# Mamba head stage: squares summed per group on GpSimd, output products one head later, decay clamp on VectorE, six biased exponentials on ScalarE

## The reference

```
proj  = x @ in_proj_w.T                      # gate, hidden, B, C, dt
hbc   = silu(causal conv of 4 taps + bias)   # hidden -> X, B, C
dt    = softplus(dt + dt_bias);  A_bt = -exp(A_log) * dt
L     = exp(cumsum difference of A_bt), lower triangle
y     = (C B^T * L) @ (X * dt) + D * X       # written in chunks in the reference
g     = y * silu(gate)
g     = g * rsqrt(mean over the group's 512 channels of g*g + 1e-6)
x     = layernorm(x + (norm_w * g) @ out_proj_w.T)
```

## Time and profile before

| what | us |
|---|---|
| median of three executions | 3315.8 |
| the three | 3315.8, 3317.79, 3304.01 |
| the profiled execution | 3299.21 |
| its span in the profile | 3297.4 |
| PE busy in the span | 2619.4 (79%) |
| DVE busy | 1809.8 (55%) |
| ACT busy | 1525.4 (46%) |
| POOL busy | 1227.2 (37%) |

### The profile page before, as it was taken

The page is one execution under the profiler, slowest core; times in us unless marked ns, Lnnn a source line. Parts: engine busy times, 40 slices in busy tenths (PEclk is TensorE's granted clock), DMA queues, the critical chain, the costliest instruction groups (busy, mean ns, idle before and its releaser), DMA issues. The chain is left out here.

```text
span 3297.4 us, 47157 instructions
## 1 busy us (share of the span) xinstructions
PE 2619.4 (79%) x13661; PEld 1670.5 (51%) x13663; DVE 1809.8 (55%) x3839; ACT 1525.4 (46%) x2975; POOL 1227.2 (37%) x1164
## 2 busy tenths in 40 slices
PE   4799999987999996577777937878557749698884
PEld 2467777744777775344444523333244414365552
DVE  4666666674666664788882146776223342133234
ACT  3555555564555552588891114655235410233321
POOL 0477777635777773000000020000000027344443
PEclk8999999998999997666657957999679868799997
DMA  1121211002221210740000000000000024587885
GB/s 61 52 52 33 59 48 36 14 14 58 58 52 33 58 26 26 250 136 1 1 1 31 0 18 1 1 1 1 23 0 0 0 81 158 129 177 172 175 172 126
DMA packets 127073, 192.74 MB, mean 58 GB/s; under 512 B 17552, under 2 KB 88208, under 8 KB 125584
## 3 DMA queue, kind: packets, MB, share of 16 engines
q1 hardware_dynamic: 83696, 134.71, 14.5%
q0 software_dynamic: 23616, 33.24, 5.8%
q10 hardware_dynamic: 19584, 22.57, 2.5%
HBM read 123.23 MB, written 67.25 MB: 58 GB/s over the span
## 5 line engine op out<-in xcount | busy, mean ns | idle before, releaser
L234 DVE SCALAR_TENSOR_TENSOR h_pre<-h_px,h_par,h_pre 128x510 f32<-128x510 f32 (+2 forms) x384 | 286.5, 746 | 269.1 <-ACT h_pre L695 249.2
L658 PE MATMUL h_po<-h_wo,h_h 128*128 128x256 f32 x1024 | 328.2, 411 | 0.0
L580 POOL TENSOR_SCALAR h_decay<-h_cumb,h_sel 128x256 f32<-128x256 f32 x256 | 290.9, 1136 | 25.2 <-DMA h_cumb<-cum_rows 25.2
L591 POOL TENSOR_TENSOR h_mix<-h_decay,cb 128x768 f32<-128x768 f32 x128 | 232.8, 1819 | 165.0 <-ACT h_decay L681 165.0
L2890 POOL DMA_INDIRECT moe_sums<-ex_y,ex_sidx x132 | 204.8, 1552 | 234.7 <-DVE ex_y L3069 216.6
L622 PE MATMUL h_px<-x_cols,h_w 128*128 128x512 f32 x512 | 254.4, 620 | 25.3 <-DMA h_d<-d_skip 25.3
L849 POOL TENSOR_TENSOR norm_rstd<-norm_mv,mhalf 128x4 f32<-128x4 f32 x24 | 28.3, 1178 | 605.3 <-DVE norm_mv L832 605.3
L627 PE MATMUL h_pz<-x_cols,h_w 128*128 128x512 f32 x512 | 242.5, 596 | 5.6 <-DVE h_gate L748 5.6
L707 ACT ACTIVATE h_xt<-h_pxt,h_sel 128x128 f32<-128x128 f32 x512 | 145.9, 368 | 151.9 <-PE h_pxt L646 151.9
L2942 PE MATMUL ex_pg<-ex_w,ex_xT 128*128 x528 | 194.7, 492 | 25.6 <-ACT ex_xT L2998 10.5
L660 PEld LDWEIGHTS h_pss<-ones,h_sq 128*128 128x128 f32 x1024 | 194.6, 190 | 26.3
(11 more groups left out here) (389 smaller groups left out, 5809.6 us busy)
## 6 DMA issues: line engine op xcount, KB each, us to landing
h_cumb<-cum_rows SPq DMA_DIRECT2D x32, 1024.0 KB, 8.6
moe_tiles<-blank SPq DMA_DIRECT2D x4, 6642.0 KB, 44.2
ex_w<-moe_w SPq DMA_DIRECT2D x64, 352.0 KB
ex_xg<-moe_tiles ACTq DMA_DIRECT2D x136, 162.0 KB, 2.6
ex_wd<-moe_wd SPq DMA_DIRECT2D x64, 176.0 KB
h_w<-w_xg SPq DMA_DIRECT2D x8, 1024.0 KB, 10.5
moe_sums<-blank SPq DMA_DIRECT2D x2, 2176.0 KB, 26.6
h_wo<-w_out SPq DMA_DIRECT2D x8, 512.0 KB, 10.3
```

The costliest lines, as they stand in the source:

```text
L234: ins = dve.scalar_tensor_tensor(out=out[:, :, back:S], in0=src[:, :, 0:S - back], scalar=par[:, at + CK - 1 - back:at + CK - back], in1=o ...
L580: pool.tensor_scalar(decay[j][:, u, 0:S], cumb[s.vb][:, j, u, :], sel[s.vb][:, u * TPB, 1, j:j + 1], 0.0, ALU.subtract, ALU.min)
L591: pool.tensor_tensor(mix[j % 2][:], decay[j][:], cbj, ALU.mult).then_inc(matched, 1)
L658: pe.matmul(po[t // TPB][:, t % TPB, :], hh[j % 2][:, t * P:(t + 1) * P], w_out[s.pg][:, j, :], start=(j == 0 and t % TPB == 0), stop=(j = ...
```

## The change

The loops and LEAD go: all 64 slots of a half are written out, and a wait whose count would be zero or less is left out (`after`). The memsets of `h_po` and `h_pss` go with them. The rest moves work between engines and slots:

- Squares: ACT squares head 0 of a step into `h_sqs` and the others into `h_sq`; POOL adds the three into `h_sqs` (`total`, 128x512); PE then makes one set of four one-column products per step.
- Output: PE's `out` goes from head k to head k-1; `h_h` gets four buffers instead of two; `out` no longer waits for a square.
- Variance and addition of the step before go from slot j = 0 to slot j = 1, the addition to the end of that slot.
- Decay: DVE takes the minimum of the broadcast sums and the row's own sum on the two diagonal blocks (`argue`, one 128x512 instruction); ACT takes six exponentials of 128 columns with the negated row sum as bias (`h_less`, made in `select`), and reads the off-diagonal block directly from `h_cumb`.
- POOL scales `h_wo` half a group ahead, for the first group before anything else.

```diff
-            parts = ((3, project), (1, scan), (2, turn), (0, out))
+            parts = ((3, project), (1, scan), (2, turn), (-1, out))
+            head_slots(-3, 1, lambda k: slot(parts, k))
...
             def out(s, j, h):
-                pe.wait_ge(finished, LEAD + h + 1)
-                pe.wait_ge(squared, LEAD + h + 1)
+                pe.wait_ge(finished, h + 1)
                 if j == 0:
-                    pe.wait_ge(added, LEAD + s.n)
-                    pe.wait_ge(scaled, LEAD + s.g + 1)
+                    after(pe, added, s.n)
+                    pe.wait_ge(scaled, s.g + 1)
                 for t in range(TW):
-                    pe.matmul(po[t // TPB][:, t % TPB, :], hh[j % 2][:, t * P:(t + 1) * P], w_out[s.pg][:, j, :],
-                              start=(j == 0 and t % TPB == 0), stop=(j == HG - 1), skip_group_check=True)
-                    mm = pe.matmul(pss[:, t:t + 1], sq[j % 2][:, t * P:(t + 1) * P], r.ones[:, 0:1],
-                                   start=(j == 0 and t == 0), stop=(j == HG - 1), skip_group_check=True)
+                    mm = pe.matmul(po[t // TPB][:, t % TPB, :], hh[j][:, t * P:(t + 1) * P], w_out[s.pg][:, j, :],
+                                   start=(j == 0 and t % TPB == 0), stop=(j == HG - 1), skip_group_check=True)
                 mm.then_inc(outed, 1)
+                if j == HG - 1:
+                    pe.wait_ge(totalled, (s.n + 1) * (HG - 1))
+                    after(pe, vared, s.n)
+                    for t in range(TW):
+                        mm = pe.matmul(pss[:, t:t + 1], sqs[s.vb][:, t * P:(t + 1) * P], r.ones[:, 0:1], start=True, stop=True)
+                    mm.then_inc(pooled, 1)
...
+            def total(s, j, h):
+                if j:
+                    pool.drain()
+                    pool.wait_ge(squared, h + 1)
+                    pool.tensor_tensor(sqs[s.vb][:], sqs[s.vb][:], sq[j % 2][:], ALU.add).then_inc(totalled, 1)
...
             def decays(s, j, h):
-                act.wait_ge(argued, LEAD + h + 1)
-                act.activation(decay[j][:], decay[j][:], ACT.Exp).then_inc(decayed, 1)
+                act.wait_ge(argued, h + 1)
+                for u in range(2):
+                    act.activation(decay[j][:, u, P:S], cumb[s.vb][:, j, u, P:S], ACT.Exp, bias=less[s.vb][:, u * TPB, j:j + 1])
+                    for b in range(TPB):
+                        own = decay[j][:, u, 2 * b * P:(2 * b + 1) * P]
+                        ins = act.activation(own, own, ACT.Exp, bias=less[s.vb][:, u * TPB + b, j:j + 1])
+                ins.then_inc(decayed, 1)
...
+            def argue(s, j, h):
+                dve.wait_ge(cums[s.vb], (s.g * (NP // 2) + s.two + 1) * 16)
+                after(dve, matched, h - HG + 1)
...
+                dve.tensor_tensor(own, cum, lim, ALU.min).then_inc(argued, 1)
...
-            def body(prev, cur, nxt):
-                for j in range(HG):
-                    finish(*head(cur, nxt, j))
-                    if j == 0:
-                        variance(prev)
-                    slot(((2, silu),), cur, nxt, j)
-                    if j == 0:
-                        if nxt:
-                            select(nxt)
-                        add(prev)
-                    slot(((3, conv), (3, open_)), cur, nxt, j)
+            def body(k):
+                n, j = divmod(k, HG)
+                slot(((0, finish), (2, silu)), k)
+                if j == 0 and n + 1 < len(STEPS):
+                    select(STEPS[n + 1])
+                if j == 1 and n >= 1:
+                    variance(STEPS[n - 1])
+                slot(((3, conv), (3, open_), (3, argue)), k)
+                if j == 1 and n >= 1:
+                    add(STEPS[n - 1])
```

More of the change, by code:

```diff
@@ L414, with __init__, head_slots, at_head @@
 class Step:
[L417 to L442, removed]
+    def __init__(self, n):
+        self.n = n
+        self.g, self.p = divmod(n, NP)
+        self.g2, self.pg = divmod(self.g, 2)
+        self.two, self.vb = divmod(self.p, 2)
+STEPS = [Step(n) for n in range(GH * NP)]
+def head_slots(first, last, body):
+    for k in range(first, len(STEPS) * HG + last):
+        body(k)
+def at_head(h):
+    return (STEPS[h // HG], h % HG, h) if 0 <= h < len(STEPS) * HG else None
 def mamba_heads(nc, a, r, half, cum_rows, dtc, cb):
@@ L522, in mamba_heads, with slot, group @@
         block = ctx2.enter_context(nc.Block())
[L524 to L529, removed]
+        def slot(parts, k):
             for ahead, part in parts:
-                at = head(cur, nxt, j + ahead)
-                if at:
-                    part(*at)
+                if at_head(k + ahead):
+                    part(*at_head(k + ahead))
         @block.sync
         def _(sp):
-            def group(g2, pg):
-                sp.wait_ge(added, LEAD + (g2 * 2 + pg - 1) * NP)
-                g = (g2 * 2 + pg) * 2 + half
+            def group(s):
+                pg = s.pg
+                after(sp, added, (s.g - 1) * NP)
+                g = s.g * 2 + half
                 sp.dma_start(w_in[pg][:], a["w_xg"][g]).then_inc(loaded[pg], 16)
@@ L573, in group @@
                                    ALU.mult).then_inc(scaled, 1)
[L575 to L584, removed]
@@ L606, in _ @@
[L606 to L609, removed]
+            def body(k):
+                if k % (HG * NP) == HG * NP // 2 and k // HG + NP // 2 < len(STEPS):
+                    group(STEPS[k // HG + NP // 2])
+                slot(((2, match), (-1, total)), k)
+                if k % HG == 1 and k > HG:
+                    root(STEPS[k // HG - 1])
+            group(STEPS[0])
@@ L611, in _ @@
+            head_slots(-2, 1, body)
+            root(STEPS[-1])
         @block.tensor
         def _(pe):
[L613 to L614 removed]
             def project(s, j, h):
[L617 removed]
+                if s.p == 0 and j == 0:
                     pe.wait_ge(loaded[s.pg], (s.g2 + 1) * 64)
[L620 removed]
+                after(pe, convolved, h - 1)
@@ L689, in activate @@
+            def square(s, j, h):
+                act.wait_ge(finished, h + 1)
+                if j == 0:
+                    after(act, pooled, s.n - 1)
+                    act.activation(sqs[s.vb][:], hh[j][:], ACT.Square).then_inc(squared, 1)
+                else:
+                    after(act, totalled, s.n * (HG - 1) + (0, 0, -1, 1)[j])
+                    act.activation(sq[j % 2][:], hh[j][:], ACT.Square).then_inc(squared, 1)
             def activate(s, j, h):
-                if s.opens and j == 0:
+                if s.p == 0 and j == 0:
```

146 lines of the change are left out of this document (59 added, 87 removed).

## The result

| | us, median | lowest to highest | runs |
|---|---|---|---|
| before, beside it | 3313.78 | 3304.01 to 3318.04 | 10 |
| after | 3330.74 | 3324.33 to 3336.10 | 10 |

The ratio is 1.0056, 95% interval [1.0043, 1.0068]: slower by 0.56%, 17 us. The profiled execution took 3328.39 us, with a span of 3326.4 (3297.4 before).

The account below looks back on a forecast made before the run. PE alone was taken to set the pace in the head stages. Work, waits, filling and tail gave -9 us, half clock +24, so +15 on the median 3315.8: forecast 3330 us, likeliest case 3313 to 3347, 8-in-10 range 3288 to 3375.

Parts of the forecast that it names:

- PE's work: In the head stages, slots shorten from 7.80 to 6.94 us, plus 0.86 per step; alone, 32 steps give back 83 us.
- The wait: PE's first output product of a step waits 2.82 us for DVE's late addition, eating the whole gain.
- The chain: From a slot's first projection through tap, conv, gate, minimum and addition until PE starts: 8.08 us.
- What is hidden: ACT's six exponentials (0.285 each), DVE's minimum and POOL's adds fit beside PE's slot; at worst 10 us in all.
- The clock: PE runs at half clock after half of the 28 stream waits, adding 24 us; the ends are none and 48.
- B: Every PE wait is followed by half clock: 3355 us, up to 3390; chance 0.24.
- C: PE's wait is there but its clock never falls: 3307 us; chance 0.15.
- D: PE's wait is absent or short: 3228 us, or 3268 with half of it; chance 0.16.
- Filling and tail: At each half's start and end: filling 7.1 us shorter, tail 1.7 us longer.
- the wait of step 15: The last step's PE wait, left out of the 14 counted per half because it lies in the tail.
- Rival E: POOL blocks DVE's minimum through SBUF reads, making the wait 4.6 us with half clock each time: 3406 us; chance 0.03.

Follow-up runs that it names:

- the fifth experiment: Changed kernel with output, sums, variance and addition in their old slots, addition ahead of conv, and one-column products per head without POOL's sums: 3297.14 us, 0.9974 of before.
- The first experiment: Changed kernel with DVE's addition ahead of the slot's conv and POOL's power ahead of its product: 3228.62 us, ratio 0.9755 against the kernel before.
- the seventh experiment: Changed kernel with POOL's product of decays and B-C products replaced by a memset that reads nothing from SBUF: 3322.91 us, one run.

## Why the prediction was right, point by point

- **PE's work.** Slots 6.90 and a set of 0.82 were 6.94 and 0.86 in the prediction; the fifth experiment prices the removed products at 77 us (predicted 83).
- **The wait.** The chain from the slot's first projection (396.30) to PE's start (404.49) is 8.19 (predicted 8.08), with the gate's and minimum's pitches 0.59 and 0.61 (0.60 and 0.65). PE is done with the transposes at 401.13 + 0.43 = 401.56, which is 5.26 into the slot (predicted 5.26; 0.43 is their pitch in a slot without a wait). The wait is 2.93 from start to start (2.82), 2.65 and 2.76 as the profile counts it (2.65). The first experiment shows the cause: with the addition and the power that it needs at earlier places the wait is gone. In the kernel after the power, at 399.33 on POOL, was done at 400.34 and hidden, as predicted; it comes into the chain only once the addition is early.
- **What is hidden.** The six exponentials below start 0.29 apart (two in 404.23 - 403.65 = 0.58), 1.74 together; 0.285 each was predicted. That they and DVE's minimum are hidden is seen in the fifth experiment, which has both: PE is busy 460 of 460 us there. These are ACT's rows in the kernel after.

```profile
403.36 0.41 ACT L653 ACTIVATE h_decay<-h_cumb,h_less 128x128 f32<-128x128 f32 x1
403.65 0.70 ACT L656 ACTIVATE h_decay<-h_decay,h_less 128x128 f32<-128x128 f32 x2
404.23 0.40 ACT L653 ACTIVATE h_decay<-h_cumb,h_less 128x128 f32<-128x128 f32 x1
404.52 0.69 ACT L656 ACTIVATE h_decay<-h_decay,h_less 128x128 f32<-128x128 f32 x2
```

- **The clock.** Half of the 28 stream waits, 24 us, was a guess between none and all; it was 12 of 28. Filling the waits gave back 21. Rivals B and C fall by this; D falls by the 83.7 us of waiting. (B's upper end of 3390 was a slip: twice the 48 for the clock gives 3316 - 9 + 96 = 3403. Nothing else rested on it.)
- **Filling and tail: two terms mis-sized, with opposite signs.** Filling was -8.8 instead of -7.1 per half, of which the next slot (to 180.22, 8.43 long instead of 6.90) takes back 1.5. The tail was +5.4 instead of +1.7: I had set the wait of step 15 apart as lying in the tail and then not charged it there, and had counted POOL's power as early, which does not hold in the tail, where the addition stands 2.97 for it. PE's wait there is 3.28 long and followed by half clock (the output products behind it take 3.56 instead of 1.88): with 1.7 for the clock that is 5.0, and with the 1.7 of the prediction, which was worked out from no row, 6.7, against 5.4 measured.
- **Rival E was refused for a wrong reason.** I took from before's `h_h`, never over 0.88, that a busy POOL does not block DVE. The mechanism exists: 2.30 against 0.68, and 0.69 beside a memset. This is the rule of the Trainium skill, page SBUF — State Buffer, section Who interferes with whom, as the prediction told it, and the traces of after and of the seventh experiment agree with it. Its price was small for another reason: in this kernel it mostly hits `h_xs`, behind the addition, where DVE has slack. The minimum's longest is 1.84, but the one in the chain above took 0.68. Where the two meet is settled by the order, so before's rows could not exclude it.

The forecast was 3330, and 3330.7 was measured, slower by just over the 0.5% that the prediction counted as no change. Part of that closeness is luck, since the misses in filling and tail partly cancel and the term for the clock was a choice. That the gain of 77 and the loss of 102 nearly cancel is not luck: the first is fixed by the removed passes, the second by the chain.

## What to carry to other kernels

When a consumer is moved a slot later, look for what releases it: it needs a new place too, and its price is what stands ahead of it on an engine that takes its work in order. Here a late addition on DVE and a late power on POOL cost 102 us together, all of the gain and more; mending the addition's alone gave back 45. Work that relieves an engine nobody waits for is worth nothing by itself and can still be what makes another edit pay: without the sums on POOL, the kernel with the decay moved gained 13 us (3310 to 3297), none of them in the stream; with the sums the move bought 127.

## What the runs showed of the hardware

- Idles of PE of the same length are not followed by the same clock: 2.76 at 404.49 by 1.00, 2.65 at 435.89 and 2.76 at 532.15 by 0.50. In the stream most half-clock stretches follow every second wait (they begin at 242.7, 307.5, 372.4 and 437.2). What sets the alternation was not tried.
- `scalar_tensor_tensor` with two SBUF inputs on DVE stood until an SBUF-reading product on POOL was done (2.30 against 0.68), and not for a memset.
